# Attention of a convolution and RWKV-style kernel: residual added in PSUM by an identity product, sum copied and squared by ScalarE

## The chip, the cores and the metric

The kernel runs on one core of one Trainium2 chip. The metric is the device time of one execution in microseconds. Before the change it is 5809.89 us, the median of three runs (5807.37 to 5811.38).

## The reference

Sixteen images of 192 channels and 56 x 56 pixels pass through a convolution block (a pointwise product, a 13 x 13 depthwise convolution, batch norms, gelu) and then through a block with attention and a feed-forward part. The change lies in the attention, of which this is what matters:

```python
tok = x.reshape(B, C, T).transpose(0, 2, 1)          # the residual
xs = _ln(tok, ln1_g, ln1_b)
xi = _omni(...)                                      # depthwise mixing
k, v, sr = xs2 @ att_wk.T, xs2 @ att_wv.T, sigmoid(xs2 @ att_wr.T)
v = _wkv(decay0, first0, k, v)                       # scan along rows
v2 = _wkv(decay1, first1, k2, v2)                    # scan along columns
att_out = sr * v @ att_wo.T
tok = tok + gamma1 * att_out                         # changed here
xf = _ln(tok, ln2_g, ln2_b)                          # needs sums and sums of squares of tok
```

`_wkv` is a recurrence over 3136 positions with a running maximum, a numerator and a denominator.

## The kernel before

The program is a chain of blocks, each for all sixteen images: preparation, the pointwise product, the 13 x 13 depthwise convolution, norm and mixing ("omni1"), the attention, norm and mixing again, the feed-forward part. Between them the images lie in DRAM. All arithmetic is float32; a float32 matmul stands in the trace as two instructions.

**The attention block** (`attention`, L820) holds two images at a time as three tiles of 128 channels by 3136 pixels (channels 0 to 127 of either image, and the last 64 channels of both together). A step takes one tile; there are 24 steps and two at the end for what is left. A step has 14 units of work, positions 0 to 13: seven are the rows phase of the step's own tile (`ROWS_AT`: positions 3, 5, 6, 8, 9, 11, 12), seven the columns phase of the tile before. Each unit covers 448 pixels. Step s is of kind s mod 3: kind 0 turns and projects the low channels of the first image and transposes two operands (`turns` 2), kind 1 projects the ends of both (`turns` 1, two half products and one whole for each of k, v and r), kind 2 the low channels of the second (`turns` 0).

Each engine has its own queue, written out by hand:

- TensorE (L1015): in a step, for t from 0 to 6: `project` (k, v, r of 448 pixels, L1026, into two banks in turn), `turn` (transposes for t + 2, L1017), and `project_out(image, t - 2)` (L1043) of the image whose two tiles are done. Groups 5 and 6 come at the end. A group is two pairs; a pair is two products q, each of two matmuls (L1054, L1055), in one of two banks `out_ps`. Only steps of kind 0 and 1 from step 3 on, and steps 24 and 25, have such an image (`finished`, L948).
- ScalarE (L1082), at each position: k read from PSUM (`evacuate`, L1102), `input_factor` (L1107) of the next unit, v read, `decay_factor` (L1112) of the next unit, r read, `log` (L1118), `mix` (L1091), `invert` (L1123), `mix`. The reads of k, v, r for t stand two positions ahead of the rows unit t: positions 1, 3, 4, 6, 7, 9, 10. Then `squares` (L1125) of a group: four squares of 192 channels with their sum, each from the finished token in SBUF, each waiting for the one before. They stand one position after VectorE's add; groups 5 and 6 stand together at the step's end.
- VectorE (L1236), for each unit: `sums` (two scans, L1262), `outputs` (L1278 to L1298), `run_max` (a scan, L1257, and L1250 or L1256) of the unit two ahead, and at `RESIDUAL_AT` (positions 5, 7, 8, 10, 11, 12, 13) `add_residual` (L1301) of one group: two adds (L1307) of 112 x 386, PSUM plus `Y`, into `Y`.
- GpSimd (L1182): exponents, products and divisions of the scans.
- SyncE (L970): loads. `store(image)` (L993) waits for the squares, writes tokens and sums, waits for them, and loads the next image's residual into the one buffer `Y` ("residual_pairs", L844: 112 partitions, 193 channels with the channel sum, 28 column pairs, so that neighbouring channels lie 112 bytes apart).

The wait that frees a bank of `out_ps` is in `project_out`, on VectorE's add two pairs before:

```python
need(pe, tok_done, image * (PJ // 2) + jp - 1)
```

Of the kernel before, what the change touches and what calls it, by code (L numbers as in the profile page):

```python
# [16 lines left out]
ALU = mybir.AluOpType  # L17
ACT = mybir.ActivationFunctionType
AX_X = mybir.AxisListType.X

C = 192
# [8 lines left out]
PJ = W // 2  # L30
K13, K5, K3 = 13, 5, 3
PITCH = 62
PXC = 2 * W
PXP = PITCH + W
JC = 4
NCH = PJ // JC
# [783 lines left out]
def attention(nc, B, keep, mix_d, y_d, sy_d, tok_d, s1_d, s2_d):  # L820
# [8 lines left out]
    TILES = 3 * (B // 2)  # L829
    XR = NCH + 2  # L830
    CY = C + 1
    with ExitStack() as ctx:
# [22 lines left out]
        tok_done = m.sem("tok_done")  # L855
# [31 lines left out]
        def need(eng, sem, value):  # L887

            if value > 0:
                eng.wait_ge(sem, value)  # L890
# [57 lines left out]
        def finished(step):  # L948

            pair, kind = divmod(step - 3, 3)  # L950
            return 2 * pair + kind if step >= 3 and kind < 2 else None

        def group_at(step, position):

            if step == TILES:
                return position - 1 if position > 0 else None
            return RESIDUAL_AT.index(position) if position in RESIDUAL_AT else None
# [13 lines left out]
        def _(sp):  # L971
# [19 lines left out]
                sp.dma_start(Y[:, C, :], dram(sy_d, image * PJ, [[B * PJ, PXC], [1, PJ]])).then_inc(y_loaded, 16)  # L991

            def store(image):  # L993
                sp.wait_ge(sq_done, PJ * (image + 1))
                sp.dma_start(groups(tok_d, image, 0, NG), in_groups(Y[:, 0:C, :], NG)).then_inc(stored, 16)
                for d, t in ((s1_d, Y[:, C, :]), (s2_d, s2[:, :])):
                    sp.dma_start(dram(d, image * PJ, [[B * PJ, PXC], [1, PJ]]), t).then_inc(stored, 16)
                sp.wait_ge(stored, 48 * (image + 1))
                if image + 1 < B:
                    load_y(image + 1)  # L1000
# [15 lines left out]
        def _(pe):  # L1016
# [26 lines left out]
            def project_out(image, group):  # L1043
                pair, n = divmod(image, 2)
                att = [rS[:, tile % 4, :] for tile in (3 * pair + 2 * n, 3 * pair + 1)]
                if group == 0:
                    pe.wait_ge(wkv_done, unit_of[3 * pair + 1 + n, False, NQ - 1].count())
                for jp in (2 * group, 2 * group + 1):

                    need(pe, tok_done, image * (PJ // 2) + jp - 1)  # L1050
                    for q in range(2):
                        j = 2 * jp + q
                        to = o_ps[jp % 2][0:PXC, q * CY:(q + 1) * CY]
                        pe.matmul(to, att[0][:, PXC * j:PXC * (j + 1)], keep.wo[:, 0, :], start=True, stop=False)  # L1054
                        mm = pe.matmul(to, att[1][:, PXC * j:PXC * (j + 1)], keep.wo[:, 1 + n, :],  # L1055
                                       start=False, stop=True)
                    mm.then_inc(out_ps_ready, 1)

            for step in range(TILES + 2):
# [23 lines left out]
        def _(act):  # L1083
# [38 lines left out]
                act.wait_ge(ln_done, unit.count())  # L1122
                act.activation(e, e, ACT.Exp, scale=-1.0).then_inc(rec_done, 1)  # L1123

            def squares(image, group):  # L1125
                for j in range(JC * group, JC * (group + 1)):
                    act.wait_ge(tok_done, image * (PJ // 2) + j // 2 + 1)
                    need(act, sq_done, image * PJ + j)
                    act.activation(junk[:, :], Y[:, 0:C, j], ACT.Square, accum_out=s2[:, j:j + 1]
                                   ).then_inc(sq_done, 1)  # L1130

            act.preload_act_table_set("natural_log_exp_and_others")
            for step in range(TILES + 1):
# [15 lines left out]
                for unit in steps[step]:  # L1149
# [19 lines left out]
                        for half in range(2):  # L1169
                            mix(step, 1, half)  # L1170
                    if done is not None:
                        group = group_at(step, unit.position - 1)
                        if group is not None:
                            squares(done, group)
                if done is not None:
                    if step == TILES:
                        squares(done, NCH - 2)
                    squares(done, NCH - 1)
            for group in range(NCH):
                squares(B - 1, group)  # L1180

        @block.gpsimd  # L1182
        def _(pool):
# [53 lines left out]
        def _(dve):  # L1237
# [60 lines left out]
                dve.scalar_tensor_tensor(grid(e), part_of(rS, unit), 1.0, Q.rearrange("p (a b) -> p a b", b=W),  # L1298
                                         ALU.add, ALU.mult).then_inc(d_done, 1)

            def add_residual(image, group):  # L1301
                if group == 0:
                    dve.wait_ge(y_loaded, 32 * (image + 1))
                for jp in (2 * group, 2 * group + 1):
                    dve.wait_ge(out_ps_ready, image * (PJ // 2) + jp + 1)
                    y = Y[:, :, 2 * jp:2 * jp + 2]
                    dve.tensor_tensor(y, o_ps[jp % 2][0:PXC, 0:2 * CY].rearrange("p (q c) -> p c q", q=2), y, ALU.add  # L1307
                                      ).then_inc(tok_done, 1)

            for n in range(2):  # L1310
                run_max(line[n])
            for step in range(TILES + 1):
                done = finished(step)
                for unit in steps[step]:
                    sums(unit)
                    outputs(unit)
                    if near(unit, 2) is not None:
                        run_max(near(unit, 2))
                    if done is not None:
                        group = group_at(step, unit.position)  # L1320
                        if group is not None:
                            add_residual(done, group)
            add_residual(B - 2, NCH - 1)
            for group in range(NCH):
                add_residual(B - 1, group)


def feed_forward(nc, B, ins, keep, mix_d, tok_d, out):
# [429 lines left out]
```

## Time and profile before

| | us |
|---|---|
| median of three runs | 5809.89 |
| lowest and highest | 5807.37, 5811.38 |
| the profiled execution, its own time | 5813.4 |
| its span | 5811.6 |
| TensorE busy | 4955.2 |
| VectorE busy | 3771.1 |
| GpSimd busy | 3556.7 |
| ScalarE busy | 3493.3 |
| granted TensorE clock, mean | 0.94 of 2.4 GHz |

The profile is one execution. Busy time of an engine is the union of its instructions; an engine may wait within a stage and be full in another, so shares of the whole span say little. A bracket behind a row is the idle time before it and the instruction that ended it. PE is TensorE, PEld its weight loads, DVE VectorE, ACT ScalarE, POOL GpSimd, SPq the queue of SyncE. L1307 is line 1307 of the kernel.

### The profile page before, as it was taken

How to read it: one execution, taken by the hardware profiler on the slowest of the kernel's cores; microseconds unless marked ns; L12 is line 12 of the kernel's file. 1: busy time of each engine (PE TensorE's matmuls, PEld its weight loads, DVE VectorE, ACT ScalarE, POOL GpSimd, SP SyncE). 2: the span in 40 equal slices, each digit the busy share in tenths (PEclk: the TensorE clock that was granted, in tenths of full speed). 3: DMA queues.
4: the chain of work that ended last, by engine and by line, in shares of the span. 5: the costliest groups of instructions: out<-in, count | busy, mean ns of one | idle time of the engine just before them, and what ended most of it. 6: DMA issues, size and time to landing. Idle time of an engine off the chain costs nothing. (4 is left out here: it accounts for less than half of the span.)

```text
span 5811.6 us, 78329 instructions
## 1 busy us (share of the span) xinstructions
PE 4955.2 (85%) x23504; PEld 3915.4 (67%) x23504; DVE 3771.1 (65%) x5591; ACT 3493.3 (60%) x6892; POOL 3556.7 (61%) x2992
## 2 busy tenths in 40 slices
PE   5979999979966776766867764997999999999999
PEld 5969999967733343443433434776888888888888
DVE  4423333367769999999999994774555555555555
ACT  0017777746656776766767764665555556665555
POOL 0027777757768888888888882775444444444444
PEclk9989999989988888988989887998999999999999
DMA  6987777689830321312223115997223223222320
GB/s 167 264 209 198 184 197 183 163 208 260 249 84 20 82 56 45 84 45 73 67 55 80 45 34 142 263 263 183 56 56 89 56 58 84 60 56 72 73 55 25
DMA packets 388598, 674.50 MB, mean 116 GB/s; under 512 B 21117, under 2 KB 346702, under 8 KB 368910
## 3 DMA queue, kind: packets, MB, share of 16 engines
q1 hardware_dynamic: 334768, 514.71, 38.1%
q10 hardware_dynamic: 53522, 156.21, 7.2%
q8 instruction: 130, 2.13, 0.1%
q14 instruction: 178, 1.46, 0.1%
HBM read 437.00 MB, written 233.87 MB: 115 GB/s over the span
## 5 line engine op out<-in xcount | busy, mean ns | idle before, releaser
L1545 POOL TENSOR_TENSOR hidden_part<-hidden_whole,hidden_part 128x448 fp32r<-128x448 f32 x672 | 752.8, 1156 | 1030.7 <-ACT hidden_part L1510 1029.9
L676 POOL TENSOR_TENSOR omni_in_part<-omni_norm,omni_in_part 113x448 fp32r<-113x448 f32 x384 | 609.1, 1598 | 202.7 <-ACT omni_in_part L735 199.7
L1414 PE MATMUL f_out_ps<-hidden_part,ffn_wv_parts 128*128 128x448 f32 (+1 forms) x3360 | 721.5, 370 | 0.7 <-POOL hidden_part L1545 0.7
L1414 PEld LDWEIGHTS f_out_ps<-hidden_part,ffn_wv_parts 128*128 128x128 f32 (+1 forms) x3360 | 578.6, 177 | 103.9 <-POOL hidden_part L1545 33.5
L1588 DVE TENSOR_SCALAR hidden_whole<-f_hid_ps 128x448 f32<-128x448 f32 x672 | 417.6, 622 | 254.2 <-POOL hidden_part L1545 149.3
L1038 PE MATMUL proj_ps<-mixT_low,kvr_weights_low 128*128 128x448 f32 x672 | 360.9, 622 | 214.7 <-ACT k_all L1102 184.1
L87 PE MATMUL omni_ps<-omni_in_part,omni_band_part 113*112 113x448 f32 x1152 | 438.8, 381 | 113.0 <-POOL omni_in_part L676 78.9
L1040 PE MATMUL proj_ps<-mixT_ends,kvr_weights_ends 128*128 128x448 f32 x1008 | 519.7, 599 | 0.0
L87 PE MATMUL dw_ps<-dw_in_part,dw_band_part 112*112 112x432 f32 (+3 forms) x1344 | 474.4, 353 | 42.6 <-POOL dw_in_part L477 42.6
L1203 POOL TENSOR_TENSOR input_times_v<-input_factor,v_all 128x448 f32<-128x448 f32 x336 | 420.3, 1251 | 93.2 <-ACT input_factor L1107 74.3
L88 PE MATMUL dw_ps<-dw_in_part,dw_band_part 112*112 112x432 f32 (+3 forms) x1344 | 474.7, 353 | 0.0
L89 PE MATMUL dw_ps<-dw_in_part,dw_band_part 112*112 112x432 f32 (+3 forms) x1344 | 472.0, 351 | 0.0
L473 POOL TENSOR_TENSOR dw_band_part<-dw_band,dw_band_part 112x784 fp32r<-112x784 f32 x192 | 335.0, 1745 | 191.9 <-ACT dw_band_part L516 191.8
L88 PE MATMUL omni_ps<-omni_in_part,omni_band_part 113*112 113x448 f32 x1152 | 436.8, 379 | 0.0
L89 PE MATMUL omni_ps<-omni_in_part,omni_band_part 113*112 113x448 f32 x1152 | 436.4, 379 | 0.0
L494 DVE TENSOR_TENSOR dw_sums<-dw_sums,dw_out 112x448 f32<-112x448 f32 x192 | 121.5, 633 | 456.6 <-ACT dw_out L545 456.6
L1414 PE MATMUL f_hid_ps<-ffn_mixT_part,ffn_wk_high 128*128 128x448 f32 x1344 | 397.3, 377 | 7.6 <-DVE hidden_whole L1588 6.2
L1510 ACT ACTIVATE hidden_part<-hidden_whole 128x448 fp32r<-128x448 f32 x672 | 389.2, 579 | 21.3
L516 ACT ACTIVATE dw_band_part<-dw_band 112x784 fp32r<-112x784 f32 x192 | 163.6, 852 | 390.8 <-DMA dw_band<-flat 383.8
L1040 PEld LDWEIGHTS proj_ps<-mixT_ends,kvr_weights_ends 128*128 128x128 f32 x1008 | 194.9, 207 | 278.7 <-issue 278.7
L1508 ACT ACTIVATE hidden_whole<-hidden_whole 128x448 f32<-128x448 f32 x672 | 379.8, 565 | 3.6 <-DVE hidden_whole L1588 2.0
L1038 PEld LDWEIGHTS proj_ps<-mixT_low,kvr_weights_low 128*128 128x128 f32 x672 | 134.8, 213 | 359.8 <-ACT k_all L1102 218.6
(178 smaller groups left out, 13181.4 us busy)
## 6 DMA issues: line engine op xcount, KB each, us to landing
xin<-x SPq DMA_DIRECT2D x16, 2352.0 KB, 13.1
x_pointwise<-xp ACTq DMA_DIRECT2D x16, 2352.0 KB, 18.8
dw_in<-x_pointwise SPq DMA_DIRECT2D x24, 1568.0 KB, 24.4
y_gelu<-dw_out ACTq DMA_DIRECT2D x24, 1568.0 KB, 13.2
omni_in<-y_gelu SPq DMA_DIRECT2D x24, 1568.0 KB, 23.0
att_mix<-omni_out ACTq DMA_DIRECT2D x24, 1568.0 KB, 12.7
residual_pairs<-y_gelu SPq DMA_DIRECT2D x16, 2352.0 KB, 11.8
tok<-residual_pairs SPq DMA_DIRECT2D x16, 2352.0 KB, 9.0
```

Source lines behind the costliest of these rows:

```text
L87: pe.matmul(bank, w_hi, x_hi, start=start, stop=False)
L88: pe.matmul(bank, w_hi, x_lo, start=False, stop=False)
L89: return pe.matmul(bank, w_lo, x_hi, start=False, stop=stop)
L676: pool.tensor_tensor(rounded(inner(p[1])), z[u][:, :, cc, :], inner(p[0]), ALU.subtract).then_inc(in_split, 1)
L1038: pe.matmul(to[:, 0:TC], keep.w_low[:, o, 0:LOW], low[kind // 2], start=True, stop=False)
L1040: pe.matmul(to[:, 0:TC], keep.w_end[:, o, part * 128:(part + 1) * 128], x_end[:, t, :], start=False, stop=True).then_inc(bank_ready, 1)
L1203: pool.tensor_tensor(grid(EV[unit.slot % 2]), grid(E[unit.slot]), part_of(vS, unit), ALU.mult).then_inc(ev_done, 1)
L1414: return pe.matmul(bank, rounded(w), rounded(x), start=start, stop=stop)
L1508: act.activation(whole[h % KW][:, :], whole[h % KW][:, :], ACT.Square).then_inc(kk_ready, 1)
L1510: act.activation(rounded(kk[n % 2][0][:, h, :]), whole[h % KW][:, :], ACT.Copy).then_inc(kh_ready, 1)
L1545: pool.tensor_tensor(rounded(kk[n % 2][1][:, h, :]), whole[h % KW][:, :], kk[n % 2][0][:, h, :], ALU.subtract).then_inc(kl_ready, 1)
L1588: dve.tensor_scalar_max(whole[h % KW][:, :], hidden_bank(n, h)[:, 0:TC], 0.0).then_inc(relu_done, 1)
```

## The change

`project_out` adds a third matmul to each product: the identity as the stationary operand, `Y[:, :, j]` as the moving one, so that the bank holds output plus residual. It waits for the residual's load ahead of group 0, and for ScalarE's squares, not for VectorE's add, before it takes a bank again. `squares` becomes `tokens`: ScalarE copies a pair from PSUM to `Y` and squares each half from PSUM. It stands one position earlier in ScalarE's queue. VectorE's `add_residual` is gone. The store waits for the copies too.

```diff
             def store(image):
+                sp.wait_ge(tok_done, (PJ // 2) * (image + 1))
                 sp.wait_ge(sq_done, PJ * (image + 1))
...
+                if group == 0:
+                    pe.wait_ge(y_loaded, 32 * (image + 1))
                 for jp in (2 * group, 2 * group + 1):
 
-                    need(pe, tok_done, image * (PJ // 2) + jp - 1)
+                    need(pe, sq_done, image * PJ + 2 * (jp - 1))
...
-                        mm = pe.matmul(to, att[1][:, PXC * j:PXC * (j + 1)], keep.wo[:, 1 + n, :],
-                                       start=False, stop=True)
+                        pe.matmul(to, att[1][:, PXC * j:PXC * (j + 1)], keep.wo[:, 1 + n, :],
+                                  start=False, stop=False)
+
+                        mm = pe.matmul(to, keep.ident[0:PXC, 0:PXC], Y[:, :, j], start=False, stop=True)
...
-            def squares(image, group):
-                for j in range(JC * group, JC * (group + 1)):
-                    act.wait_ge(tok_done, image * (PJ // 2) + j // 2 + 1)
-                    need(act, sq_done, image * PJ + j)
-                    act.activation(junk[:, :], Y[:, 0:C, j], ACT.Square, accum_out=s2[:, j:j + 1]
-                                   ).then_inc(sq_done, 1)
+            def tokens(image, group):
+                for jp in (2 * group, 2 * group + 1):
+                    act.wait_ge(out_ps_ready, image * (PJ // 2) + jp + 1)
+                    bank_of = o_ps[jp % 2]
+                    act.activation(Y[:, :, 2 * jp:2 * jp + 2],
+                                   bank_of[0:PXC, 0:2 * CY].rearrange("p (q c) -> p c q", q=2), ACT.Copy
+                                   ).then_inc(tok_done, 1)
+                    for q in range(2):
+                        j = 2 * jp + q
+                        need(act, sq_done, image * PJ + j)
+                        act.activation(junk[:, :], bank_of[0:PXC, q * CY:q * CY + C], ACT.Square,
+                                       accum_out=s2[:, j:j + 1]).then_inc(sq_done, 1)
...
-                        group = group_at(step, unit.position - 1)
+                        group = group_at(step, unit.position)
                         if group is not None:
-                            squares(done, group)
-                if done is not None:
-                    if step == TILES:
-                        squares(done, NCH - 2)
-                    squares(done, NCH - 1)
+                            tokens(done, group)
+            tokens(B - 2, NCH - 1)
             for group in range(NCH):
-                squares(B - 1, group)
+                tokens(B - 1, group)
...
-            def add_residual(image, group):
-                if group == 0:
-                    dve.wait_ge(y_loaded, 32 * (image + 1))
-                for jp in (2 * group, 2 * group + 1):
-                    dve.wait_ge(out_ps_ready, image * (PJ // 2) + jp + 1)
-                    y = Y[:, :, 2 * jp:2 * jp + 2]
-                    dve.tensor_tensor(y, o_ps[jp % 2][0:PXC, 0:2 * CY].rearrange("p (q c) -> p c q", q=2), y, ALU.add
-                                      ).then_inc(tok_done, 1)
```

## Rows read from the trace of the kernel before

**Rows 1.** The page, part 2: VectorE's busy tenths in forty slices.
```profile
DVE  4423333367769999999999994774555555555555
```

**Rows 2.** Stretches: length, busy PE, PEld, DVE, ACT, POOL (instructions), clock, DMA, GB/s.
```profile
1768.20:1840.40 72.20, 39.80 (x92) 19.25 (x91) 70.13 (x105) 41.88 (x78) 65.15 (x63) 0.75 0.00 0
...
2054.40:2133.50 79.10, 59.69 (x228) 39.05 (x228) 74.92 (x116) 57.05 (x125) 67.43 (x65) 0.88 0.18 41
2133.60:2212.90 79.30, 65.19 (x266) 34.32 (x266) 76.85 (x120) 60.25 (x140) 64.75 (x63) 0.91 0.34 82
2213.00:2286.50 73.50, 43.42 (x108) 21.83 (x108) 71.98 (x110) 48.56 (x101) 64.99 (x63) 0.83 0.26 67
```

**Rows 3.** TensorE's timeline in step 6: start us, us, matmuls merged.
```profile
2091.76 0.49 PE L1054 MATMUL out_ps<-attention_out_weights,r_all 128*112 128x193 f32 x2
...
2094.38 0.91 PE L1038 MATMUL proj_ps<-mixT_low,kvr_weights_low 128*128 128x448 f32 x2
...
2098.89 0.61 PE L1022 MATMUL proj_ps<-identity,mix_low 112*128 112x112 f32 x4
...
2107.38 0.61 PE L1022 MATMUL proj_ps<-identity,mix_low 112*128 112x112 f32 x4
...
2108.75 0.49 PE L1054 MATMUL out_ps<-attention_out_weights,r_all 128*112 128x193 f32 x2
...
2115.50 1.02 PE L1038 MATMUL proj_ps<-mixT_low,kvr_weights_low 128*128 128x448 f32 x2 [0.96 <-ACT k_all L1102]
...
2126.88 0.49 PE L1055 MATMUL out_ps<-attention_out_weights,r_all 128*112 128x193 f32 x2
```

**Rows 4.** Waits in step 6: who waited for whom, us, times, longest us.
```profile
ACT k_all L1102 <- PE proj_ps L1040: 4.4, 3, 3.1
...
PE proj_ps L1022 <- ACT mixT_low L1091: 17.1, 1, 17.1
```

**Rows 5.** The adds: duration ns min/median/max, first and last start us, form.
```profile
L1307 DVE TENSOR_TENSOR residual_pairs<-out_ps,residual_pairs x224: 522/548/571, 1864.1 to 3549.0; 112x386 f32<-112x386 f32 x112
```

**Rows 6.** ScalarE: strided SBUF, unstrided SBUF, strided PSUM; columns as in rows 5.
```profile
L1129 ACT ACTIVATE tok_squares<-residual_pairs x448: 537/561/587, 1869.6 to 3552.1; 112x192 f32<-112x192 f32 x150
...
L1484 ACT ACTIVATE ffn_wr_parts<-ffn_wr x1: 347/347/347, 4010.8 to 4010.8; 128x192 fp32r<-128x192 f32 x1
...
L746 ACT ACTIVATE omni_out<-omni_ps x384: 517/536/549, 1214.3 to 3989.7; 112x448 f32<-112x448 f32 x192
```

**Rows 7.** Weight loads in the timeline: a strided operand, then an unstrided one.
```profile
2083.89 0.55 PEld L1022 LDWEIGHTS proj_ps<-identity,mix_low 112*128 112x128 f32 x4 [0.58 <-ACT v_all L1102]
...
2085.78 0.30 PEld L1038 LDWEIGHTS proj_ps<-mixT_low,kvr_weights_low 128*128 128x128 f32 x2 [0.35 <-ACT mixT_low L1091]
```

**Rows 8.** ScalarE's timeline in step 6.
```profile
2101.67 0.57 ACT L1129 ACTIVATE tok_squares<-residual_pairs 112x192 f32<-112x192 f32 x1
...
2128.71 0.54 ACT L1129 ACTIVATE tok_squares<-residual_pairs 112x192 f32<-112x192 f32 x1
...
2131.49 0.56 ACT L1107 ACTIVATE input_factor<-input_factor 128x448 f32<-128x448 f32 x1
...
2134.07 0.55 ACT L1129 ACTIVATE tok_squares<-residual_pairs 112x192 f32<-112x192 f32 x1
```

**Rows 9.** Step 7 in the timeline: the residual's load, then TensorE.
```profile
2158.15 4.23 SPq L991 DMA_DIRECT2D residual_pairs<-y_sums  x1
...
2170.05 0.49 PE L1054 MATMUL out_ps<-attention_out_weights,r_all 128*112 128x193 f32 x2
...
2186.85 0.61 PE L1022 MATMUL proj_ps<-identity,mix_low 112*128 112x112 f32 x4
...
2187.30 0.49 PE L1054 MATMUL out_ps<-attention_out_weights,r_all 128*112 128x193 f32 x2
...
2194.78 0.97 PE L1035 MATMUL proj_ps<-mixT_low,kvr_weights_low 128*64 128x448 f32 x4 [1.00 <-ACT k_all L1102]
```

**Rows 10.** VectorE's timeline at the first units of step 7.
```profile
2148.77 1.16 DVE L1262 TENSOR_TENSOR_SCAN sums_state<-decay_factor,sums_last,input_factor 128x448 f32<-128x448 f32 x1 [0.77 <-ACT decay_factor L1112]
```

More of the change, by code:

```diff
@@ L1312, in _ @@
             for step in range(TILES + 1):
-                done = finished(step)
                 for unit in steps[step]:
@@ L1318, in _ @@
                         run_max(near(unit, 2))
[L1319 to L1325, printed above, removed]
 def feed_forward(nc, B, ins, keep, mix_d, tok_d, out):
```

## The prediction

> **What bounds the kernel now.** I began with the page's forty slices, since the shares of the whole span mix stages: from slice 13 to slice 24 VectorE stands at 9 tenths [rows 1], and that is the attention. Then stretches one step long, cut at VectorE's memsets of L1250: step 2, without token work, lasts 72.2 us; step 6 lasts 79.1, step 7 79.3, step 8 73.5 [rows 2]. Steps 6 and 7 are of kind 0 and 1 and carry an image's residual, step 8 is of kind 2 and carries none; these three stand seven times (steps 3 to 23), and step 24 carries a fifteenth image.
>
> In step 6 VectorE is busy 74.9 of 79.1 us, ScalarE 57.0, TensorE 59.7 [rows 2]. The easy reading: VectorE is the limit, and seven groups of two adds cost the 7 us between step 2 and step 6. The order of TensorE's work tells more. From group 0 of the output product at 2091.76 to the end of group 4 at 2127.4 it has one hole, 0.96 us at 2115.50 [rows 3]. The 75% over the step hides this, because TensorE stands still for 17.1 us at the step's start, until ScalarE has turned the mix; and ScalarE waits 4.4 us for k in the same step [rows 4]. So from position 4 to 10 TensorE keeps just the pace of VectorE: both are full.
>
> **The change, part by part.**
> *VectorE* loses 224 adds of 548 ns [rows 5], two of which take 1.0 us together with their overlap: 7 us a residual step, if nothing else holds it.
>
> *TensorE* gets 448 identity products, each two instructions of 193 columns like those beside it. A group's 16 instructions take from 2091.76 to 2094.38, 2.62 us, 0.164 each [rows 3]; 24 take 3.93, so 1.31 more a group. The new operand is read from residual_pairs with 112 bytes from one element to the next, and no matmul here streams such an operand. From below: no penalty, 0.164. From above: what ScalarE pays at that stride, 561 ns for 192 elements against 347 side by side [rows 6], 1.1 ns an element more, thus some 0.37 us an instruction. I take 0.164, for the nearest row is TensorE's own weight load of mix_low at that stride: four loads of 0.21 in 0.55 us, one every 0.113; two unstrided ones of 0.19 in 0.30, one every 0.11 [rows 7].
> The Trainium skill ("Advanced Engine Details and Errata", Memory Cachelines) says that SBUF wants two hits on each 16-byte line for full speed and costs more otherwise: by that rule the identity product is slow, and the sum some 100 us higher than by the row of the loads. ScalarE's squares agree with it, TensorE's weight loads do not.
>
> *ScalarE* now copies 112x386 from PSUM and squares from PSUM. Four squares with what follows take 2.78 us now (2128.71 to 2131.49 [rows 8]). Unstrided, each is about 0.21 us shorter [rows 6]. The copy: 448 elements from PSUM, read 64 bytes apart, take 536 ns [rows 6], so 386 take 0.48, of which some 0.08 overlaps. Its output goes in pairs 112 bytes apart; from above 1.1 ns an element more, 0.9 us. VectorE writes that same pattern from PSUM in 548 ns [rows 5], near what ScalarE needs for more elements, so I take 0.48. A group costs 2.78 - 0.84 + 2 x 0.40 = 2.7, say 2.6 to 2.8: ScalarE's load stays.
>
> *Waits.* A bank is free after ScalarE's second square, no longer after VectorE's add, and behind it in TensorE's queue stand the projections that ScalarE itself needs next. ScalarE's group stands one position earlier than its squares did; ahead of it may be a wait for the product, behind it the next two exponentials, which VectorE's scans need. TensorE also waits for the residual's load ahead of group 0, with all later projections behind that: in step 7 the load's last part is issued at 2158.15 and lands about 12 us later, 2170.1, while group 0 starts at 2170.05 [rows 9]. The store that precedes it moves with the step, so I put nothing on this, at most 1 us. The store's extra wait is on copies that are done before the squares: nothing.
>
> **The sum, kind 0 (step 6).** Ahead of project 6, whose k is read at position 10, stand groups 0 to 3: 4 x 1.31 = 5.2, less the hole of 0.96, +4.3. Then the new wait. Project 4 ends at 2107.4 now [rows 3], 2110.0 behind two longer groups. After it ScalarE does r, log, mix, invert, mix, 2.8 us (from 2098.89, where project 3 ends, to the square at 2101.67 [rows 3, 8]), and only then group 1, whose first pair is squared at 2110.0 + 2.8 + 1.3 = 2114.1. TensorE is due to begin group 2 at 2108.75 + 2.62 = 2111.4 [rows 3]: it waits 2.7, and projects 5 and 6 behind it. So project 6 comes 7.0 later, and VectorE, 1.0 a group lighter, waits for its k. From there ScalarE sets the pace: 5.0 a position (2.65 for a group, 2.35 for the four exponentials and logs) against 5.36 now (2128.71 to 2134.07 [rows 8]); four positions give back 1.5. The seam gives back 0.8, the wait that eight squares in a row cause at 2148.77 [rows 10]. **+4.7 us.**
> **Kind 1 (step 7).** 4 x 1.31 less its hole of 1.00 [rows 9], +4.2. Group 2 is due at 2187.30 + 2.62 = 2189.9; project 4 ends at 2186.85 + 2.62 = 2189.5, plus 2.3 (one mix fewer), plus 1.3 = 2193.1: a wait of 3.2. Less the same 2.3: **+5.1.**
> **Kind 2:** nothing. **Step 24 and the last image:** no projections there, so six groups leave VectorE, -6, and a burst of eight squares becomes one group, -3. Then 14 pairs of 12 instructions, 1.97 each, where four half pairs of squares set 1.48: +7, and 2 for filling. Zero together.
> Sum: 7 x (4.7 + 5.1) = 69. The profiled execution took 5813.4 us around its span of 5811.6, 3.5 above the median: 5813.4 + 69 - 3.5 = 5879.
>
> **The rivals.**
> *TensorE has room, and VectorE's work comes off.* Residual steps fall to 72 or 73: 15 x 7 = 105 off, 5705; half of it if TensorE trails a little, 5757. For: VectorE is 95 to 97% busy in both kinds [rows 2]. Against: TensorE without room in rows 3. It decides if 1.31 a group fits before the k that VectorE needs; I see 1.0 of 5.2. Chance 0.15.
> *It cancels.* No wait in group 2 (ScalarE comes earlier than I count), +4.3, and the tail gives back VectorE's four last groups, 4.0: +0.3 a step, 5814. Chance 0.10.
> *The strided operand is slow.* At 0.37 an instruction a group costs 1.65 us more than in my sum, 4 x 1.65 x 14 = 92, and 11 in the last image: 5982. For: ScalarE pays it [rows 6]. Against: TensorE's loads do not [rows 7]. Chance 0.13. The line rule of the Trainium skill (Memory Cachelines, as above) is this case.
> *The copy is slow, or the square no shorter.* 0.8 us more a group; ScalarE is full from position 7 on, which five groups feel: 4.0 x 14 = 56, 5935. Chance 0.08.
> *My forecast*, 5840 to 5920: 0.54.
>
> **How the numbers follow.** Slower by over 0.2% (about the least that runs of this kernel can tell from no change): 0.54 + 0.13 + 0.08, 0.75. Within it: 0.10. Faster: 0.15. The range holds the forecast, the cancelling case, the slow copy and the milder half of the two far cases, 5757 and a partly slow operand: 5760 to 5975.
>
> **What would show it.** Right: steps 6 and 7 at 83 to 86 us between their memsets, step 8 still 73; the 17 us hole at the start kept, and a new hole of 2 to 3 us before group 2, ended by a square; ScalarE's longest wait for k over 4 us, at position 7 or 10; VectorE waiting for k and the decay factor in positions 7 to 11; the identity product at the pitch of its neighbours; squares near 0.33 us, copies near 0.48. Wrong: steps 6 and 7 at 73 (the first rival), identity products with more than 0.164 us from one to the next, or copies near 0.9.

## The result, and the profile of the changed kernel

The changed kernel takes 6017.05 us (median of four runs, 6013.24 to 6017.53); beside them the kernel before took 5808.63 (5806.41 to 5811.38). The ratio is 1.0357, interval 1.0344 to 1.0371: slower by 208 us. The direction was forecast, the size was not: 5879 with a range up to 5975. The profiled execution has a span of 6015.3 us against 5811.6.

The page, part 1, and VectorE's busy tenths in part 2 [rows 1]:

```profile
PE 5247.7 (87%) x24400; PEld 4105.6 (68%) x24400; DVE 3677.0 (61%) x5367; ACT 3474.0 (58%) x7116; POOL 3548.1 (59%) x2992
...
DVE  4423333377598878788887875676555555555555
```

VectorE has 94 us less to do than before (3771.1), TensorE 292 more, and VectorE's nines in the attention have become sevens and eights but for one. The stretches of steps 6, 7 and 8 answer to [rows 2]; the columns are the same:

```profile
2082.70:2174.20 91.50, 71.30 (x248) 46.28 (x249) 71.19 (x106) 56.18 (x135) 66.10 (x64) 0.86 0.15 36
2174.30:2268.50 94.20, 83.17 (x327) 45.21 (x326) 71.15 (x106) 59.45 (x154) 65.81 (x64) 0.98 0.28 69
2268.70:2341.40 72.70, 50.27 (x141) 26.78 (x139) 70.03 (x104) 48.18 (x104) 65.35 (x64) 0.87 0.26 67
```

Step 6 takes 91.5 us where it took 79.1, step 7 94.2 for 79.3, step 8 72.7 for 73.5. At the last column memset, 3643.30 against 3447.13, 196 of the 204 us between the two spans are lost, and the last image adds 8. Steps 6 to 8 stand for the others: over the seven of each kind the mean rises from 79.1 to 91.5, from 79.4 to 95.0 and from 73.7 to 73.9. In step 6 VectorE is now busy 71.2 of 91.5 us; the waits of that step say for whom it stands still (who waited for whom, us, times, longest; compare [rows 4]):

```profile
PE proj_ps L1023 <- ACT mixT_low L1096: 15.9, 1, 15.9
ACT k_all L1107 <- PE proj_ps L1041: 15.8, 6, 6.0
DVE run_max L1264 <- ACT k_all L1107: 10.8, 3, 4.4
...
DVE sums_state L1270 <- ACT decay_factor L1117: 7.4, 7, 1.6
...
PE out_ps L1057 <- ACT tok_squares L1140: 5.1, 2, 2.9
```

VectorE waits for k, k is late because ScalarE waits 15.8 us for projections (4.4 before), and TensorE waits for ScalarE's squares. TensorE's timeline in step 6, group 0, then the starts of groups 2 and 4 (answering to [rows 3]):

```profile
2119.51 0.49 PE L1057 MATMUL out_ps<-attention_out_weights,r_all 128*112 128x193 f32 x2
2119.84 0.49 PE L1058 MATMUL out_ps<-attention_out_weights,r_all 128*112 128x193 f32 x2
2120.17 0.87 PE L1061 MATMUL out_ps<-residual_pairs,identity 112*112 112x193 f32 x2
2120.86 0.51 PE L1057 MATMUL out_ps<-attention_out_weights,r_all 128*112 128x193 f32 x2
...
2124.94 0.56 PE L1039 MATMUL proj_ps<-mixT_low,kvr_weights_low 128*128 128x448 f32 x1
...
2144.55 0.58 PE L1057 MATMUL out_ps<-attention_out_weights,r_all 128*112 128x193 f32 x2 [2.23 <-ACT tok_squares L1140]
...
2168.71 0.58 PE L1057 MATMUL out_ps<-attention_out_weights,r_all 128*112 128x193 f32 x2 [2.86 <-ACT tok_squares L1140]
```

From 2119.51 to 2119.84 two instructions of 193 columns take 0.33 us, 0.165 each, as before. The identity product takes from 2120.17 to 2120.86, 0.69 for its two: 0.345 each. The group takes 5.43 us where it took 2.62. The wait before group 2 is there as forecast, 2.23 us; the one before group 4 was not forecast. The forms (ns min/median/max; compare [rows 5, 6]):

```profile
L1061 PEld LDWEIGHTS out_ps<-residual_pairs,identity x896: 174/177/311, 1857.8 to 3761.4; 112*112 112x112 f32 x180
L1061 PE MATMUL out_ps<-residual_pairs,identity x896: 512/531/540, 1857.9 to 3761.7; 112*112 112x193 f32 x180
```
```profile
L1134 ACT ACTIVATE residual_pairs<-out_ps x224: 502/526/553, 1861.1 to 3762.3; 112x386 f32<-112x386 f32 x112
```
```profile
L1140 ACT ACTIVATE tok_squares<-out_ps x448: 305/331/357, 1861.5 to 3763.1; 112x192 f32<-112x192 f32 x150
```

The squares are at 0.33 us as expected, the copies at 0.53, a little over the 0.48 taken.

### The profile page after: what moved, and what is told of

It is laid out like the page before. It is cut to its first block and busy times, and to the rows that moved or that the text cites. A ratio compares the mean times of both kernels' runs of the same rounds, so it can differ in the third digit from the quotient of the medians.

```text
span 6015.3 us, 79675 instructions
## 1 busy us (share of the span) xinstructions
PE 5247.7 (87%) x24400; PEld 4105.6 (68%) x24400; DVE 3677.0 (61%) x5367; ACT 3474.0 (58%) x7116; POOL 3548.1 (59%) x2992
## 5 line engine op out<-in xcount | busy, mean ns | idle before, releaser
L1270 DVE TENSOR_TENSOR_SCAN sums_state<-decay_factor,sums_last,input_factor 128x448 f32<-128x448 f32 x288 | 329.3, 1144 | 142.0 <-ACT decay_factor L1117 141.9
L1061 PE MATMUL out_ps<-residual_pairs,identity 112*112 112x193 f32 x896 | 389.0, 524 | 0.0
```

Source lines behind the costliest of these rows:

```text
L1061: mm = pe.matmul(to, keep.ident[0:PXC, 0:PXC], Y[:, :, j], start=False, stop=True)
```

## The experiments

Eighteen kernels were run, each beside the kernel before (5808 to 5810 us). Line numbers are those of each kernel. Some kernels leave the residual out or add it twice; the text says which. Lengths of steps are read from the column memsets of each trace, and the length of a group runs from its first instruction's start to its last one's end.

### What the identity product costs

**Side by side.** The moving operand is a weight tile without a stride (so the residual is left out and weights are added instead).

```diff
-mm = pe.matmul(to, keep.ident[0:PXC, 0:PXC], Y[:, :, j], start=False, stop=True)
+mm = pe.matmul(to, keep.ident[0:PXC, 0:PXC], keep.wo[0:PXC, 2 - n, :], start=False, stop=True)
```

> The changed kernel, but the identity product streams 193 weights that lie side by side instead of the residual at 112 bytes from element to element; the residual is left out of the sum and a block of weights added in its place, while all waits and counts of instructions stay. Theory (the strided operand takes 0.37 us an instruction instead of 0.16, and TensorE is full from position 4 on): identity instructions 0.164 us apart, a group back from 5.6 to 3.9 us, steps 6 and 7 near 84 us instead of 91.6 and 94.3, 5870 to 5900 us in all. Rival (the stride costs little, and the time went into the new waits between TensorE and ScalarE): 5960 us or more.

Measured 5928.35 us, ratio 1.0206 (1.0186 to 1.0226): the stride costs 89 us, and 120 remain. That is over the theory's 5870 to 5900 and under the rival's 5960, so each named only a part of the loss. Between the kernel after and this one 77 us lie ahead of the last column memset and 11 in the last image.

**Pairs.** The whole computation, with one identity product for both halves of a bank, so that each 112-byte step brings two neighbouring values.

```diff
+pe.matmul(o_ps[jp % 2][0:PXC, 0:2 * CY].rearrange("p (q c) -> p c q", q=2),
+          keep.ident[0:PXC, 0:PXC], Y[:, :, 2 * jp:2 * jp + 2], start=True, stop=False)
...
-mm = pe.matmul(to, keep.ident[0:PXC, 0:PXC], Y[:, :, j], start=False, stop=True)
```

> The changed kernel with one identity product for both halves of a pair, placed first: it streams 386 elements, two neighbouring ones (8 bytes) at each step of 112 bytes, and writes them to the two halves of the bank in turn, 772 bytes apart. The same sum as the changed kernel. Theory (two elements on each line take the penalty away, as in ScalarE's and VectorE's pairs): 0.33 us for an instruction of 386 columns, time as with operands side by side, 5870 to 5900 us. Rival (every jump of 112 bytes costs, or the write that alternates does): 0.5 us or more an instruction, 5930 to 6020 us.

Measured 5932.58, ratio 1.021 (1.0193 to 1.0227), within the noise the same as side by side. The time lies in the rival's range (5930 to 6020), because both ranges left out what the side-by-side run still loses; the row decides for the theory. The form of its identity product:

```profile
L1054 PE MATMUL out_ps<-residual_pairs,identity x448: 510/514/987, 1859.3 to 3674.4; 112*112 112x386 f32 x150
```

It has twice the columns of L1061 above at the same 112 bytes from one pair to the next, and takes 514 ns for 531: two values at each place take no longer than one. From one such instruction to the next it is 0.35 us.

**The product alone, on the kernel before**, first side by side, then with the strided residual (added twice). VectorE adds and ScalarE squares as before.

```diff
-mm = pe.matmul(to, att[1][...], keep.wo[:, 1 + n, :], start=False, stop=True)
+pe.matmul(to, att[1][...], keep.wo[:, 1 + n, :], start=False, stop=False)
+mm = pe.matmul(to, keep.ident[0:PXC, 0:PXC], keep.wo[0:PXC, 2 - n, :], start=False, stop=True)
```

> The kernel before with a third matmul in each product, identity by 193 weights side by side; VectorE's add, ScalarE's squares and all waits stay as they were, and a block of weights is added to the output's sum. It loads TensorE alone with 1.31 us a group. Theory (TensorE has 1 us of room ahead of position 10): +4 to +5 us in steps 6 and 7, 5865 to 5880 us in all. Rival (TensorE has room, VectorE is the limit): steps unchanged, 5808 to 5815 us.

> The kernel before with the identity product on the strided residual (so the residual is added twice), all else as before: the run with the side-by-side operand stood at 5870. Theory: TensorE has no room in kinds 0 and 1, so 8 instructions a group by 0.2 us, four groups, fourteen images: 90 us over that run, 5950 to 5970. Rival (part of the stride's price is hidden by TensorE's waits): 5900 to 5940.

Measured 5869.7 (1.0105, 1.0085 to 1.0125) and 5987.84 (1.0305, 1.0288 to 1.0322). The first bears out the term "4 x 1.31 ahead of project 6": the sum had 4.3 and 4.2 us a step, and steps of kind 0 are 2.9 us longer (82.0 for 79.1), those of kind 1 4.0 (83.4 for 79.4). That is 49 us in the fourteen steps; that the whole difference, 61, is so near the 60 of the two terms is in part chance, for 6 us of it lie in the last image. The second is above the ranges of both its theory and its rival: 118 us for the stride, where 8 x 0.18 x 4 groups x 14 images makes 81. 15 of the 118 lie in the last image; why the rest is over 81 is open. TensorE is so late there that ScalarE waits 181 us for k in the stretch from 1640 to 3400 (115 with the side-by-side operand).

### Without the identity product: what swallows VectorE's gain

**None.** The kernel after without the identity product (residual left out): VectorE has no adds, TensorE no extra work.

> The changed kernel without the identity product; the residual is left out of the sum. VectorE's adds are gone, ScalarE copies and squares from PSUM, and the bank is freed by the squares, as in the changed kernel. Theory (TensorE was full before the change, so VectorE's 7 us a step are only partly given back, and the wait for the squares ahead of group 2 takes about 2.5 us): steps 6 and 7 at 76 to 79 us, 5750 to 5800 us in all. Rival (VectorE alone was the limit): steps at 73 us, 5705 us. Rival (the wait for the squares is the main cost): steps over 80 us, over 5820 us.

Measured 5822.38, ratio 1.0025 (1.0011 to 1.0038): slower than before by a quarter of a percent, where the theory had 5750 to 5800. It is the second rival's case, over 5820 us and 81 us a step. So the 105 us that the prediction's first rival gave for VectorE's adds (15 x 7) were taken by something that is neither the product nor the stride. ScalarE in step 6 of this kernel:

```profile
2104.87 0.55 ACT L1094 ACTIVATE mixT_ends<-proj_ps 128x448 f32<-128x448 f32 x1
2108.55 0.54 ACT L1105 ACTIVATE k_all<-proj_ps 128x448 f32<-128x448 f32 x1 [3.14 <-PE proj_ps L1041]
```

and TensorE later:

```profile
2115.12 0.58 PE L1057 MATMUL out_ps<-attention_out_weights,r_all 128*112 128x193 f32 x2 [2.23 <-ACT tok_squares L1138]
```

ScalarE stands still for 3.1 us for k of project 4, while group 1, whose product ended at 2107.0, lies ready in its banks. Only after k, v, r, log, mix and inversion, at 2113.8, does it take the tokens, and TensorE waits for them.

**One project later**, with and without the product: the output groups stand one project later in TensorE's queue, the tokens at positions 7, 8, 10, 11, 12, 13 and the end.

> The paired identity product, with each group of output products one project later in TensorE's queue and ScalarE's tokens one place later (positions 7, 8, 10, 11, 12, 13 and the step's end). The same work as the run with pairs; only three groups instead of four stand ahead of project 6, and the group that had to wait for the squares has a position more. Theory (the new wait and the fourth group cost 3 to 5 us a step): steps of kind 0 and 1 at 81 to 84 us instead of 86 and 90, 5840 to 5870 us in all. Rival (TensorE's load alone sets the step): as the run with pairs, 5925 us or more.

> The run without the identity product (the residual is left out of the sum), with the same later places for TensorE's groups and ScalarE's tokens. TensorE's work is that of the kernel before and VectorE's adds are gone. Theory (with the adds gone, what held that run at 5822 us was the order: TensorE's wait for the squares and ScalarE's tokens ahead of its read of k): 5730 to 5770 us. Rival (ScalarE or TensorE is full whatever the order): 5810 us or more.

Measured 5923.69 (1.0194, 1.0174 to 1.0215) and 5838.44 (1.0048, 1.0032 to 1.0064). Both theories failed: the first run is at the edge of its rival (5925 or more), the second inside its own (5810 or more). Without the product TensorE waited 151 us in all for squares in the stretch from 1640 to 3660, more than in the run with the old places (114): the tokens had moved with the groups.

**Squares earlier, on the kernel before; then the bank freed by them.**

```diff
-group = group_at(step, unit.position - 1)
+group = group_at(step, unit.position)
```
```diff
-need(pe, tok_done, image * (PJ // 2) + jp - 1)
+need(pe, sq_done, image * PJ + 2 * (jp - 1))
```

> The kernel before with one thing moved: ScalarE's squares stand in the position of their own group, as the tokens do in the kernel after, not one later; VectorE still adds, and its add still frees the bank. This is the control for the next run. Theory (ScalarE and TensorE in a loop over the banks): the squares now wait for an add at the end of VectorE's position, and the exponentials of the next position stand behind them, so some time is lost by this alone: 5815 to 5850 us, with ScalarE waiting for residual_pairs. Rival (the place costs nothing, since ScalarE has 20 us to spare a step): 5805 to 5815.

> As the run before this one, and one wait changed: TensorE takes a bank again after ScalarE's squares of the pair, as in the kernel after, not after VectorE's add. Theory (the loop costs some 100 us): 50 to 110 us over the run with the add freeing the bank, with TensorE's waits for tok_squares above 70 us in all and ScalarE's for k above 120. Rival (what is lost is ScalarE's own load, and the wait takes the place of others): within 15 us of it.

Measured 5905.68 (1.0163, 1.0146 to 1.018) and 5956.46 (1.0235, 1.0207 to 1.0263): 96 us for the place alone, far over the 5 to 40 expected, and 51 more for the wait, the low end of the theory's 50 to 110 (TensorE waits 148 us for squares in the stretch from 1640 to 3660). The place costs through the read of k behind it:

```profile
2107.23 0.57 ACT L1129 ACTIVATE tok_squares<-residual_pairs 112x192 f32<-112x192 f32 x1 [1.04 <-DVE residual_pairs L1304]
...
2110.03 0.52 ACT L1102 ACTIVATE k_all<-proj_ps 128x448 f32<-128x448 f32 x1
```

Group 0's squares wait for the add, then hold k of project 3 until 2110.03, and TensorE waits for that bank in the middle of the project:

```profile
2110.60 1.02 PE L1038 MATMUL proj_ps<-mixT_low,kvr_weights_low 128*128 128x448 f32 x2 [2.56 <-ACT k_all L1102]
```

**Bank freed by the copy; copies alone.** In both, `tok_done` frees the bank again (the residual is left out). In the first the squares are read from the copied tokens, one position later, as in the kernel before; in the second there are none, but for one an image, so the sums of squares are left out too.

> The kernel after without the identity product (so the residual is left out), and with the banks freed by ScalarE's copies: the two copies of a group stand where the tokens stood, and the squares are read from the copied tokens in SBUF in their place of the kernel before, one position later. Theory (the loop): with the same work for TensorE and VectorE as in the run without the identity product (5822 us), TensorE waits 0.5 to 1 us for a copy in place of 2.2 to 2.9 for squares, and ScalarE has squares to do where it waited for k: 5745 to 5795 us. Rival (ScalarE's load: it has 0.84 us a group more, since the squares are strided again): 5820 to 5860.

> The kernel after without the identity product and without the squares (the residual and the sums of squares are left out, but for one square an image), banks freed by ScalarE's copies. ScalarE has 1.0 us a group where the run without the identity product (5822 us) has 2.34 and the run with the bank freed by the copy and strided squares (5872 us) has 3.8. Theory (ScalarE's work between its reads of k, v and r is what swallows VectorE's gain): 5705 to 5735 us, steps of kind 0 and 1 at 72 to 75. Rival (TensorE's own order and its banks hold these steps): 5780 to 5820.

Measured 5871.96 (1.0109, 1.0092 to 1.0126) and 5780.41 (0.995, 0.9933 to 0.9966). The first went the rival's way, and 12 us beyond its range: with the strided squares ScalarE's work on a group is 3.6 us (0.8 for the copies, 2.8 for the squares), where the run without the product has 2.3. The second is at the low end of the rival's range (5780 to 5820), far from the theory's 5705 to 5735: with next to no squares TensorE still waits for the copies (stretch from 1640 to 3400):

```profile
PE out_ps L1057 <- ACT residual_pairs L1132: 69.0, 42, 2.1
```

**Four banks.** The two more banks come from the decay factor, which is written over its exponent in SBUF; the first run is that alone, on the kernel before.

```diff
-A = [m.ps(f"decay_factor{u}") for u in range(2)]
+A = AX
...
-need(pool, a_exp, unit.count(2))
+need(pool, p_done, unit.count(2))
```
```diff
-need(pe, sq_done, image * PJ + 2 * (jp - 1))
+need(pe, sq_done, image * PJ + 2 * (jp - 3))
```

> The kernel before with the decay factor written over its exponent in SBUF, not to PSUM: the control for the two runs with four banks, whose two banks come from there. One theory only, that it costs little: 5800 to 5830 us.

> The whole computation, with the identity product in pairs (5933 us with two banks) and four banks for the output product, so that TensorE's group waits for squares of the group before the last. Theory (TensorE has no room whatever the banks): TensorE's waits for squares go, but its 24 us of extra products in each pair of steps stay: 5870 to 5900. Rival (the loop over two banks was most of the loss): below 5840.

> The kernel after without the identity product (residual left out; 5822 us with two banks), with four banks. Theory (ScalarE's load between its reads delays k, v, r and the exponentials, whatever the banks): 5770 to 5815. Rival (the loop over two banks swallows VectorE's gain): 5710 to 5750, steps of kind 0 and 1 at 73 to 76.

Measured 6156.08 (1.06, 1.0582 to 1.0618), 6162.3 (1.0611, 1.0593 to 1.0629) and 6133.49 (1.056, 1.0542 to 1.0577). The control itself costs 348 us, where 5800 to 5830 was expected, and even the steps of kind 2, which have no output product, take 90.9 us for 73.7; so the two runs with four banks, which lie outside all their ranges, say nothing of the banks. Besides the scans that follow, the control has GpSimd wait longer for the exponent's buffer; the two were not tried apart. Its scans on VectorE, before and with the factor in SBUF:

```profile
L1262 DVE TENSOR_TENSOR_SCAN sums_state<-decay_factor,sums_last,input_times_v x288: 1123/1134/1159, 1652.6 to 3494.2; 128x448 f32<-128x448 f32 x144
```
```profile
L1262 DVE TENSOR_TENSOR_SCAN sums_state<-decay_exponent,sums_last,input_factor x288: 1123/1326/1985, 1653.3 to 3837.9; 128x448 f32<-128x448 f32 x144
L1262 DVE TENSOR_TENSOR_SCAN sums_state<-decay_exponent,sums_last,input_times_v x288: 1126/1805/1979, 1654.3 to 3839.0; 128x448 f32<-128x448 f32 x144
```

### The place of the tokens

**Tokens of groups 1 and 3 one position sooner**, nothing else.

```diff
-RESIDUAL_AT = [5, 7, 8, 10, 11, 12, 13]
+RESIDUAL_AT = [5, 6, 8, 9, 11, 12, 13]
```

> The kernel after without the identity product (residual left out; 5822 us), with ScalarE's tokens of groups 1 and 3 one position sooner (positions 5, 6, 8, 9, 11, 12, 13 in place of 5, 7, 8, 10, 11, 12, 13), so that they stand ahead of the read of k of the next project, where ScalarE idles 3.1 and 2.5 us, and TensorE's groups 2 and 4 find their bank free. Nothing else is changed. Theory (the order of ScalarE's queue, tokens behind reads that wait for TensorE, swallows the gain): TensorE's waits for tok_squares fall from 114 us by more than half, 5755 to 5795 us. Rival (ScalarE's load holds the step): 5810 to 5830.

> The same two groups one position sooner in the whole computation with paired identity products (5933 us). Theory: TensorE's extra products stay, its waits for squares go: 5880 to 5910. Rival (TensorE is late enough that ScalarE's tokens now wait for the product and hold k): 5925 to 5960.

Without the product: 5767.59, ratio 0.9931 (0.9916 to 0.9946), 55 us less for two moved groups and inside the theory's range; TensorE's waits for squares fell from 114 to 65 us, a little less than the half that was expected. Whole computation with paired products: 5833.38, ratio 1.0043 (1.0028 to 1.0059), 99 us less than with the old places, where the theory gave 23 to 53. Its waits in the stretch from 1640 to 3660, with the old places and then with the sooner ones:

```profile
ACT k_all L1107 <- PE proj_ps L1041: 178.5, 84, 4.6
PE out_ps L1054 <- ACT tok_squares L1140: 89.9, 49, 3.4
```
```profile
ACT k_all L1107 <- PE proj_ps L1041: 61.8, 70, 3.1
PE out_ps L1054 <- ACT tok_squares L1140: 33.9, 34, 3.0
```

ScalarE in the run without the product now does group 1 where it idled:

```profile
2095.67 0.54 ACT L1094 ACTIVATE mixT_ends<-proj_ps 128x448 f32<-128x448 f32 x1
2096.54 0.54 ACT L1132 ACTIVATE residual_pairs<-out_ps 112x386 f32<-112x386 f32 x1 [0.33 <-PE out_ps L1058]
...
2099.36 0.54 ACT L1105 ACTIVATE k_all<-proj_ps 128x448 f32<-128x448 f32 x1 [0.22 <-PE proj_ps L1041]
```

k follows with a wait of 0.22 us in place of 3.14. Besides the waits there is TensorE's clock. In the side-by-side run, before and behind group 2 of step 7 (stretch, length, busy PE, PEld, DVE, ACT, POOL, granted clock, DMA, GB/s):

```profile
2208.70:2214.20 5.50, 5.50 (x20) 1.71 (x20) 1.75 (x3) 2.08 (x4) 2.37 (x3) 1.00 0.01 1
2214.70:2217.40 2.70, 0.06 (x1) 0.00 (x0) 2.70 (x7) 2.67 (x10) 1.08 (x2) 0.91 0.60 54
2217.50:2224.60 7.10, 7.10 (x24) 6.68 (x24) 4.13 (x6) 4.34 (x14) 4.09 (x5) 0.56 0.82 204
2224.70:2230.20 5.50, 5.50 (x20) 1.70 (x20) 1.79 (x3) 3.32 (x9) 2.44 (x3) 1.00 0.00 0
```

TensorE stands for 2.70 us, and the group behind it runs mostly at the lower clock (0.56 of 2.4 GHz on the mean; the lower level is 1.2): 7.2 us for what takes 4.1 elsewhere. In that run group 2 takes 5.87 us in all seven steps of kind 0, and 7.2 in six of the seven of kind 1 (5.6 in the other). And in the paired kernel with the sooner tokens, over groups 0 to 4 of step 6:

```profile
2095.20:2136.00 40.80, 40.43 (x166) 27.55 (x164) 33.60 (x52) 33.25 (x88) 30.82 (x30) 1.00 0.36 80
```

TensorE is busy 40.4 of 40.8 us at full clock, and there every group of steps 3 to 23 takes 4.18 to 4.28 us. With the same pairs and the old places, group 2 takes 5.9 us in kind 0 and 7.1 in kind 1, behind waits of 2.24 and 2.71.

**A version faster than both?** Groups 0 to 3 by VectorE's adds as before, groups 4 to 6 (which no later k waits for) and all of image 14 by paired identity products and ScalarE. First with ScalarE's part where the squares stood, then in the group's own position.

```diff
+if fused(image, jp):      # image 14, and groups 4 to 6 of images 0 to 13
+    pe.matmul(o_ps[jp % 2][0:PXC, 0:2 * CY].rearrange("p (q c) -> p c q", q=2),
+              keep.ident[0:PXC, 0:PXC], Y[:, :, 2 * jp:2 * jp + 2], start=True, stop=False)
```
```diff
-group = group_at(step, unit.position - 1)
+group = group_at(step, unit.position)      # of the fused groups alone
```

> The kernel before, with the change only where TensorE has room: groups 4 to 6 of an image, whose products stand behind project 6, and the whole image of step 24. There the residual enters the bank by one paired identity product and ScalarE copies and squares from PSUM; groups 0 to 3 and the last image keep VectorE's add and the squares from SBUF. Squares and copies keep the old places in ScalarE's queue. Theory (TensorE is full only ahead of project 6): VectorE's three groups come off in full, 2.8 us in each of 14 steps, and 5 us in step 24: steps near 76.5 us, 5765 us in all. Rival (ScalarE's order at the step's end, or TensorE's start into the next step, takes it back): 5790 to 5810 us.

> The whole computation: groups 0 to 3 of an image by VectorE's add as before, groups 4 to 6 (and all of image 14) by paired identity products and ScalarE, as in the run at 5811 us, but with ScalarE's copy and squares of the latter in their group's own position (11, 12, 13), not one later. Theory (the order of ScalarE's queue again; TensorE waited 6 us ahead of group 5): 5765 to 5795 us, which beats the kernel before. Rival (ScalarE's load after position 10 sets the end of the step): 5800 to 5820.

Measured 5811.31 (1.0002, 0.9993 to 1.0012) and 5799.7 (0.9981, 0.9972 to 0.999). The first equals the kernel before, just above its rival's 5790 to 5810 and far from the theory's 5765. The second beats the kernel before by 0.2%, short of the theory's 5795; TensorE's wait ahead of group 5 in step 6 was 6.09 us in the first and is 3.97 in the second:

```profile
2131.80 0.99 PE L1071 MATMUL out_ps<-residual_pairs,identity 112*112 112x386 f32 x1 [6.09 <-ACT tok_squares L1161]
```
```profile
2130.40 0.99 PE L1071 MATMUL out_ps<-residual_pairs,identity 112*112 112x386 f32 x1 [3.97 <-ACT tok_squares L1161]
```

What sets the remaining wait was not tried.

## Why the prediction came out low

**What held.** TensorE has next to no room from position 4 to 10 [rows 3]: the side-by-side product alone costs 2.9 and 4.0 us a step, where the sum gave it 4.3 and 4.2. The copies came to 0.53 us, the squares to 0.33, kind 2 lost nothing, the hole of some 16 us was kept, and a wait came before group 2 (2.23 us in kind 0, 2.71 in kind 1, for 2.7 and 3.2). The residual's load, put at nothing or at most 1 us, lands just late in step 7: the last part is issued at 2198.52, takes 12.4 us, and group 0 starts at 2211.01 behind an idle 0.76. Over the seven steps of kind 1 this idle time is 0 to 1.86 us, 6 in all.

**Step 1 that failed: "I take 0.164, for the nearest row is TensorE's own weight load of mix_low at that stride"** [rows 7]. A weight load is not the moving operand. The row of ScalarE [rows 6] was the better neighbour: 0.345 us measured against its 0.37, and 89 us by the side-by-side run, where the sum had nothing. The rival with the strided operand, given 0.13, was right in its mechanism and near in size: it had 92 us in the steps and 11 in the last image, and 77 and 11 were measured. Its 5982 is still 35 short, because it stood on the rest of my sum. By the line rule of the Trainium skill ("Advanced Engine Details and Errata", Memory Cachelines) a single value from each 16-byte line is slow and two are enough; both halves agree with the runs, 531 ns for 193 single values and 514 for 193 pairs. The same section says that matmuls are slowed by any access pattern in PSUM that is not contiguous; the paired product writes to places 772 bytes apart in turn and takes 0.35 us for 386 columns, where two side-by-side instructions of 193 take 0.33. The pattern in PSUM was not tried by itself.

**Step 2 that failed: the new wait.** Its length was nearly right; its price was not. (a) The sum has no term for TensorE's clock. At 1.00 from group 0 to group 4 in the kernel before, it falls behind the wait: group 2 takes 1.8 us longer in kind 0 and 3.1 in kind 1 of the side-by-side run, in the kernel after mostly 1.0 to 1.3 in both kinds. There the strided third of a group's instructions hardly felt the lower clock: behind the hole in step 6 two side-by-side instructions take 0.62 to 0.65 us in place of 0.33, two strided ones 0.70 for 0.69 at full clock:

```profile
2146.60 0.85 PE L1058 MATMUL out_ps<-attention_out_weights,r_all 128*112 128x193 f32 x2
2147.25 0.89 PE L1061 MATMUL out_ps<-residual_pairs,identity 112*112 112x193 f32 x2
2147.95 0.82 PE L1057 MATMUL out_ps<-attention_out_weights,r_all 128*112 128x193 f32 x2
```

(b) "ScalarE sets the pace ... four positions give back 1.5. The seam gives back 0.8": they gave back next to nothing. Group 4 waits 2.86 us in the same way and is slowed too, in the side-by-side run in all steps of kind 0 and in one of kind 1; that this is the reason is my reading, for no run took that wait away alone. The paired kernel with the sooner tokens agrees: there neither group 2 nor group 4 waits, the terms are 4 x 1.40 - 0.96 = 4.6 for kind 0 and 4 x 1.40 - 1.00 = 4.6 for kind 1, the steps are 2.4 and 2.3 us longer than before, and so the 2.3 of the sum are given back. For kind 0 of the side-by-side run the terms without what is given back are 4 x 1.32 - 0.96 + 2.24 + 1.76 = 8.3, measured 7.5 on the mean (86.6 against 79.1); for kind 1, 4 x 1.32 - 1.00 + 2.71 + 3.1 = 10.1, measured 11.1 (90.44 against 79.37). The forecast had 4.7 and 5.1, 62 us less over seven steps of each. Kind 2 is 1.5 us shorter there than in the kernel before, and the last image 4, which the forecast did not have: together that makes 48 of the other 50 us of the miss.

**The cause beneath (a) and (b): a place in a queue.** I treated the wait as a consequence of the bank's release and of ScalarE's load. The runs put most of it down to the order: tokens of group 1 stand behind the read of k of project 4, so ScalarE idles for k with tokens ready, and TensorE then idles for the tokens. With two entries of one list changed, 99 of the whole computation's 124 us beyond the stride are gone. In sum, of 208 us: 84 the stride (5932.58 with pairs), 99 the place of two groups (5833.38), and 25 are left, of which the product is the cost (66 us between the two runs with sooner tokens) and the gain is what the run without the product has over the kernel before (42), with VectorE's adds gone.

**Open.** How much of the 99 us is wait and how much clock was not separated: no run changed one without the other. In the two traces, a step of kind 0 is 4.8 us shorter with the sooner tokens and one of kind 1 8.3; the wait ahead of group 2 that is gone is 2.2 and 2.7 of it, the faster group 2 1.7 and 2.9. Whether more banks would help is open as well, since the two that could be had cost more than they could bring. Why moving the squares in the kernel before costs 96 us is shown at one place only.

## What to carry to other kernels

When one engine frees a buffer that another fills, look at what stands ahead of the release in its queue: work that is ready must come before a read that waits for the very engine that needs the buffer. Price a new hole on TensorE as the hole and, from above, a stretch at the lower clock behind it. Bound a strided operand by a row that reads it in the same role, and read two neighbouring elements at each place where the layout allows.

## What was not expected of the hardware

- TensorE streamed 193 single float32 values 112 bytes apart in 0.345 us an instruction against 0.165 side by side, while its weight loads at the same stride were as quick as unstrided ones [rows 7]; 193 pairs took 0.35. At the lower clock the strided single values took hardly longer (of all 896 the longest record is 540 ns, the median 531), the pairs up to 987 ns for 514.
- A hole of 2.70 us was followed by 7.1 us at a granted clock of 0.56. It is not so each time: in step 6 of the run without the product, group 2 ran at 1.00 behind a hole of 2.23 us, and group 4 at 0.67 behind one of 2.86. Over the fourteen steps of that run the clock fell in group 2 five times and in group 4 thirteen times; what decides it is not shown.
- A scan on VectorE whose factor and addend both lie in SBUF took 1805 ns at the median against 1134 with the factor in PSUM; its shortest, 1126, was as before. GpSimd's instructions grew too, the differences of L1190 from 980 to 1757 ns at the median. The Trainium skill ("SBUF — State Buffer", the section "SBUF: two separate sides") has a VectorE instruction with two SBUF inputs and a GpSimd instruction that reads SBUF take turns at a pair of ports; the two durations agree with that; a run of either engine alone was not made.
